# Delta attention's block product and merge: unpaired, with 96 weight columns, and queues drawn anew

## The reference

```python
def step(S, inp):
    qt, kt, vt, bt, gt = inp
    S = S * jnp.exp(gt)[..., None, None]
    for i in range(nh):                       # nh = 3
        ki, vi, bi = (kt[:, :, i], vt[:, :, i], bt[:, :, i])
        kS = jnp.einsum('bhd,bhde->bhe', ki, S)
        S = S + bi[..., None, None] * (ki[..., None] * (vi - kS)[:, :, None, :])
    o = jnp.einsum('bhd,bhde->bhe', qt, S)
    return (S, o)
```

## Time and profile before

| | us |
|---|---|
| median of three runs | 3138.93 |
| profiled execution | 3139.86 |
| its span, first to last instruction | 3138.0 |
| TensorE matmuls busy | 2919.0 (93%) |
| TensorE weight loads busy | 2241.5 (71%) |
| VectorE busy | 2486.9 (79%) |
| ScalarE busy | 2346.9 (75%) |
| GpSimd busy | 1977.9 (63%) |

### The profile page before, as it was taken

The page is one execution under the profiler, slowest core; times in us unless marked ns, Lnnn a source line. Parts: engine busy times, 40 slices in busy tenths (PEclk is TensorE's granted clock), DMA queues, the critical chain, the costliest instruction groups (busy, mean ns, idle before and its releaser), DMA issues. The chain is left out here.

```text
span 3138.0 us, 84065 instructions
## 1 busy us (share of the span) xinstructions
PE 2919.0 (93%) x27212; PEld 2241.5 (71%) x27212; DVE 2486.9 (79%) x5731; ACT 2346.9 (75%) x7723; POOL 1977.9 (63%) x3127
## 2 busy tenths in 40 slices
PE   5569999999999999999999999999987999768999
PEld 3448888888888888888888888888776444455444
DVE  5669999999999999999999999999754455594544
ACT  4769999999999999999999999999754443314443
POOL 1588888888888888888888888888831000100000
PEclk8779999999999999999999999999998999868999
DMA  5457777777777777777777777777532323002242
GB/s 108 123 147 179 190 187 180 180 184 174 184 187 191 182 182 182 178 179 182 193 184 182 183 179 182 180 189 181 154 96 75 152 102 152 10 3 78 107 160 115
DMA packets 588208, 482.91 MB, mean 154 GB/s; under 512 B 464784, under 2 KB 504368, under 8 KB 581632
## 3 DMA queue, kind: packets, MB, share of 16 engines
q1 hardware_dynamic: 579328, 474.39, 57.4%
q10 hardware_dynamic: 8448, 3.15, 0.4%
HBM read 285.53 MB, written 191.86 MB: 152 GB/s over the span
## 5 line engine op out<-in xcount | busy, mean ns | idle before, releaser
L953 DVE SCALAR_TENSOR_TENSOR conv_k<-PP,tk,conv_k 128x256 f32<-128x256 f32 x1536 | 718.5, 479 | 101.0 <-ACT conv_k L772 75.7
L953 DVE SCALAR_TENSOR_TENSOR conv_v<-PP,tv,conv_v 128x256 f32<-128x256 f32 x1152 | 540.5, 478 | 57.4 <-ACT conv_v L772 43.1
L710 POOL TENSOR_TENSOR X<-X,tmp 96x31 f32<-96x31 f32 (+15 forms) x992 | 534.3, 539 | 77.8
L707 POOL TENSOR_TENSOR tmp<-At,X 96x31 f32<-96x31 f32 (+15 forms) x992 | 486.7, 491 | 63.3 <-DMA At<-n_d 5.1
L1114 PE MATMUL PP<-xn,wk 128*128 128x268 f32 x1024 | 342.5, 418 | 41.4 <-DVE conv_k L953 29.7
L675 POOL TENSOR_TENSOR Sg<-S,gend 128x512 f32<-128x512 f32 x256 | 266.6, 1041 | 63.3 <-DVE S L912 63.3
L744 ACT ACTIVATE recA<-TG,es 96x128 f32<-96x128 f32 x1024 | 285.0, 367 | 6.3 <-DVE es L946 6.3
L693 POOL TENSOR_TENSOR rk<-ss,half 96x8 f32<-96x8 f32 x128 | 209.0, 1633 | 125.9 <-DVE ss L921 119.6
L1078 PE MATMUL RB<-rhs,Yf 96*96 96x128 f32 x2048 | 269.7, 274 | 18.7 <-DVE rhs L901 18.4
L772 ACT ACTIVATE conv_k<-PP,tk 128x256 f32<-128x256 f32 x512 | 245.2, 480 | 46.6 <-PE PP L1114 26.1
L1068 PE MATMUL RA<-S,kqgB 128*96 128x128 f32 x2048 | 276.1, 278 | 1.0 <-DVE S L912 1.0
(11 more groups left out here) (292 smaller groups left out, 6578.4 us busy)
## 6 DMA issues: line engine op xcount, KB each, us to landing
kqg_d<-kqgA SPq DMA_DIRECT2D x128, 512.0 KB, 6.4
kqgB<-kqg_d SPq DMA_DIRECT2D x128, 512.0 KB, 4.4
rec_d<-recA SPq DMA_DIRECT2D x128, 480.0 KB, 3.4
recB<-rec_d SPq DMA_DIRECT2D x128, 480.0 KB, 6.1
f1gates<-f1gates_d SPq DMA_DIRECT2D x24, 1024.0 KB, 6.8
f2gates<-f2gates_d SPq DMA_DIRECT2D x24, 1024.0 KB, 6.9
gdec<-gdec_d SPq DMA_DIRECT2D x128, 128.0 KB, 5.8
apk_d<-apkA SPq DMA_DIRECT2D x128, 128.0 KB, 3.3
```

Source lines behind the costliest of these rows:

```text
L707: nc.gpsimd.tensor_tensor(t, At[q % 2][:, j, j + 1:].unsqueeze(2).broadcast_to(sh), X[q % 2][:, j, 0:cols].unsqueeze(1).broadcast_to(sh), ...
L710: nc.gpsimd.tensor_tensor(x, x, t, ALU.subtract).then_inc(sub_ev, 1)
L953: return nc.vector.scalar_tensor_tensor(acc, src[:, :, j:j + SPAN], w[:, j:j + 1], acc, ALU.mult, ALU.add)
```

## The change

**Block product and merge.** `zm`, `wm` and `m3` run unit after unit. The weights of zm and wm are now 96 columns wide: a unit's 64 and the next unit's first 32, so that the output has 96 rows, of which the last 32 are never read. `apkB` and the buffer behind `Zt` get 32 more columns of zeros for the last unit. ZW has eight units on the same partitions. m3 writes 32 rows, with 32 weight columns. The copies are one per call and twice as large, two for `zev`.

```diff
-        ZW, RA, RB, SD = pb("ZW", [128, HU, 64]), ...
+        ZW, RA, RB, SD = pb("ZW", [128, U, 64]), ...
...
-                for u in paired():
-                    last = mm(spot(u, 0, 64), apkB[N % 2][:, u, :], Dd[N % 2][:, u, :], start=True, stop=True)
+                for u in range(U):
+                    last = mm(ZW[0:R, u, :], apkB[N % 2][:, 64 * u:64 * u + R], Dd[N % 2][:, u, :], start=True, stop=True)
                 last.then_inc(zm_mm, 1)
...
-                for u in paired():
-                    last = mm(spot(u, 0, 64), Zt[:, u, :], Yf[N % 2][:, u, BLK:R], start=True, stop=True)
+                for u in range(U):
+                    last = mm(ZW[0:R, u, :], ZtW[:, 64 * u:64 * u + R], Yf[N % 2][:, u, BLK:R], start=True, stop=True)
                 last.then_inc(wm_mm, 1)
...
-                for u in paired():
-                    last = mm(spot(u, 32, 64), Zt[:, u, :], Yf[N % 2][:, u, 64:96], start=True, stop=True)
+                for u in range(U):
+                    last = mm(ZW[0:32, u, 32:64], Zt[:, u, 0:32], Yf[N % 2][:, u, 64:96], start=True, stop=True)
                 last.then_inc(m3_mm, 1)
...
-                for p in range(2):
-                    nc.scalar.activation(half(Zt[32:64, :, 0:32], p), ZW[64 * p:64 * p + 32, :, 0:32], ACT.Copy, scale=-1.0)
-                    last = nc.scalar.activation(half(Zt[64:96, :, :], p), ZW[64 * p + 32:64 * p + 64, :, :], ACT.Copy, scale=-1.0)
-                last.then_inc(zev_ev, 1)
+                nc.scalar.activation(Zt[32:64, :, 0:32], ZW[0:32, :, 0:32], ACT.Copy, scale=-1.0)
+                nc.scalar.activation(Zt[64:96, :, :], ZW[32:64, :, :], ACT.Copy, scale=-1.0).then_inc(zev_ev, 1)
```

**Queues.** The loops run one pass longer, and the border of a pass lies elsewhere: f - 1 in a call below is what f was. On TensorE:

```diff
-                v_tile(c, 0)  v_tile(c, 1)  ktr(f - 1, 1)  ks(r, 0)  ktr(f - 1, 0)  zm(c)  ot(r - 1)
-                w_(r, 0)  v_tile(c, 2)  out(r - 1)  gate_tile(c)  sr(r, 0)  k_tile(f, 1)  o_(r, 0)
-                k_tile(f, 0)  wm(c)  ks(r, 1)  gram(f - 1, 0)  k_tile(f, 2)  w_(r, 1)  gram(f - 1, 1)
-                k_tile(f, 3)  o_(r, 1)  m3(c)  vtr(c, 1)  vtr(c, 0)  sr(r, 1)
+                ktr(f - 2, 1)  ks(r - 1, 0)  v_tile(c - 1, 2)  ot(r - 2)  ktr(f - 2, 0)  w_(r - 1, 0)
+                out(r - 2)  gate_tile(c - 1)  sr(r - 1, 0)  k_tile(f - 1, 1)  k_tile(f - 1, 0)  wm(c - 1)
+                ks(r - 1, 1)  gram(f - 2, 0)  k_tile(f - 1, 2)  gram(f - 2, 1)  k_tile(f - 1, 3)
+                w_(r - 1, 1)  o_(r - 1, 0)  m3(c - 1)  o_(r - 1, 1)  vtr(c - 1, 1)  v_tile(c, 0)
+                sr(r - 1, 1)  v_tile(c, 1)  zm(c)  vtr(c - 1, 0)
```

On ScalarE (the calls of a pass, new order):

```diff
+                osb_(r - 2)  ksum_(f - 2, 1)  tap0(c - 1, "v2")  ksum_(f - 2, 0)  wev(r - 1, 0)  gate_(c - 1)
+                vsilu(c - 1)  tap0(f - 1, "k1")  tap0(f - 1, "k0")  kr(f - 2, 0)  kr(f - 2, 1)
+                xt(*group_at(f - 1, 2 * GROUP + 1))  tap0(f - 1, "k2")  tap0(f - 1, "q")  w12(c - 1)
+                wev(r - 1, 1)  q2_(f - 2)  yev(c - 1)  mo_(r - 1, 0)  mo_(r - 1, 1)  tap0(c, "v0")
+                ksilu(f - 1)  qsilu(f - 1)  tap0(c, "v1")  zev(c)
```

On VectorE (new order; taps of different tiles stand between each other where they can):

```diff
+                tap2(c - 1, "v1")  rhs_(r - 1, 0)  og_(r - 2)  tap1(c - 1, "v2")  tap3(c - 1, "v1")
+                tap2(c - 1, "v2")  tap3(c - 1, "v2")  ss_(f - 2)  rinv_(f - 2)  step_(f - 2)  acc_(r - 2)
+                es_(f - 2)  sup(r - 1, 0)  tap1(f - 1, "k0")  tap2(f - 1, "k0")  tap1(f - 1, "k1")
+                tap3(f - 1, "k0")  tap2(f - 1, "k1")  tap3(f - 1, "k1")  rhs_(r - 1, 1)  ap(f - 2, 0)
+                tap1(f - 1, "k2")  ap(f - 2, 1)  tap2(f - 1, "k2")  tap1(f - 1, "q")  tap3(f - 1, "k2")
+                tap2(f - 1, "q")  tap3(f - 1, "q")  vr(c - 1, 1)  tap1(c, "v0")  sup(r - 1, 1)
+                tap2(c, "v0")  tap3(c, "v0")  tap1(c, "v1")  vr(c - 1, 0)
```

On GpSimd and SyncE:

```diff
+                sg(r - 1, 1)  subst(*group_at(f - 1, GROUP + 1), range(0, 6))  fo_(r - 1)  rk_(f - 2)  sg(r, 0)
+                x_zero(*group_at(f, 3))  subst(*group_at(f - 1, GROUP + 1), range(6, 12))  kqg(f - 1)
...
-                at_load(*group_at(f, GROUP + 1))  x_store(*group_at(f, 2 * GROUP + 1))  rec_load(c)  da_load(c + 1)
-                weights(*divmod(f, KSTEPS))  dec_load(f)  kqg_store(f - 1)  rec_store(f - 1)  ap_store(f - 1)
-                y_load(c + 1)
+                at_load(*group_at(f - 1, GROUP + 1))  dec_load(f - 1)  weights(*divmod(f + 1, KSTEPS))  tables(f + 1)
+                rec_load(c - 1)  x_store(*group_at(f - 1, 2 * GROUP + 1))  kqg_store(f - 2)  da_load(c + 1)
+                ap_store(f - 2)  rec_store(f - 2)  y_load(c)
```

```diff
-                nc.vector.tensor_tensor(kv[:, :, 0, :], kv[:, :, 0, :], end, ALU.mult)
-                nc.vector.tensor_tensor(rv[:, :, 1, :], rv[:, :, 1, :], mid, ALU.mult).then_inc(t_ev, 1)
-                dve.wait_ge(t_ev, ...)
-                nc.vector.tensor_tensor(fv[:, :, 1, :], fv[:, :, 1, :], mid, ALU.mult).then_inc(up_ev, 1)
+                nc.vector.tensor_tensor(r, r, mid, ALU.mult)
+                dve.wait_ge(kup_ev, kups[l, b] + 1)
+                nc.vector.tensor_tensor(f, f, mid, ALU.mult).then_inc(up_ev, 1)
...
+            def keys(l, b):
...
+                pool.wait_ge(up_ev, ups[l - 1, b] + 1)
+                pool.wait_ge(p_mm, products(l, b) + 1)
+                k = halves(kB, l, b)[:, :, 0, :]
+                nc.gpsimd.tensor_tensor(k, k, last_of_half(l, b, 1), ALU.mult).then_inc(kup_ev, 1)
```

More of the change, by code:

```diff
@@ L477, in half @@
             return t[:, hf * HU:(hf + 1) * HU]
[L479 to L483, removed]
         def of_cc(t, cc):
@@ L530, in wv_load, with tables @@
                 sp.dma_start(wo[h % 2][:, :], g.dram["Wo"][128 * h:128 * (h + 1), :]).then_inc(ld_wv[h % 2], 16)
+            def tables(h):
+                if 0 < h < NH:
+                    for b in range(B):
+                        keep_table(sp, h, b)
             def dec_load(N):
@@ L845, in w12 @@
                 need(act, wm_mm, N)
-                for p in range(2):
-                    last = nc.scalar.activation(half(Yf[N % 2][32:64, :, 64:96], p), ZW[64 * p + 32:64 * p + 64, :, 32:64], ACT.Copy)
-                last.then_inc(w12_ev, 1)
+                nc.scalar.activation(Yf[N % 2][32:64, :, 64:96], ZW[32:64, :, 32:64], ACT.Copy).then_inc(w12_ev, 1)
             def yev(N):
@@ L853, in yev @@
                 need(act, m3_mm, N)
-                for p in range(2):
-                    last = nc.scalar.activation(half(Yf[N % 2][0:32, :, 32:96], p), ZW[64 * p:64 * p + 32, :, :], ACT.Copy)
-                last.then_inc(yev_ev, 1)
+                nc.scalar.activation(Yf[N % 2][0:32, :, 32:96], ZW[0:32, :, :], ACT.Copy).then_inc(yev_ev, 1)
             def xt(q, k):
@@ L1675, in steps @@
                 yield "tile", i
-                for l in range(2):
-                    b, odd = divmod(i - 2 - l, 2)
-                    if not odd and 0 <= b < B - 1:
-                        yield "near", (l, b)
-            yield "near", (0, B - 1)
-            yield "near", (1, B - 1)
-            for l in range(2, LV + 1):
+                for x in WITHIN[i]:
+                    yield "near", x
+            done = [x for w in WITHIN for x in w]
+            for l in range(LV + 1):
                 for b in range(B):
-                    yield ("near" if l < MASKED else "far"), (l, b)
+                    if (l, b) not in done:
+                        yield ("near" if l < MASKED else "far"), (l, b)
         order = [x for kind, x in steps() if kind == "near"]
         near_no = {x: n for n, x in enumerate(order)}
-        ups = {}
+        ups, kups = {}, {}
         for kind, x in steps():
@@ L1880, in _ @@
                 spread(b)
-            for b in range(B):
-                far(LV, b)
+            for l, b in FAR:
+                far(l, b)
             for q in range(NG // 4):
@@ L1899, in _ @@
                 nc.gpsimd.memset(P[:, 4 * i:4 * i + 4, :, :], 0.0).then_inc(cleared, 1)
+            def keys(l, b):
+                if not l:
+                    return
+                pool.wait_ge(up_ev, ups[l - 1, b] + 1)
+                pool.wait_ge(p_mm, products(l, b) + 1)
+                k = halves(kB, l, b)[:, :, 0, :]
+                nc.gpsimd.tensor_tensor(k, k, last_of_half(l, b, 1), ALU.mult).then_inc(kup_ev, 1)
+            nc.gpsimd.memset(mhalf[:, :], -0.5).then_inc(mhalf_ev, 1)
+            pool.wait_ge(mhalf_ev, 1)
+            root(0)
+            for kind, x in steps():
+                if kind == "tile":
+                    root(x + 1)
+                else:
+                    keys(*x)
         @block.vector
```

287 lines of the change are left out of this document (151 added, 136 removed).

## The result

The changed kernel takes 3384.17 us (median of 4 runs, 3381.02 to 3388.69); the kernel before, run beside it, 3139.14. The ratio is 1.078, 95% interval 1.076 to 1.080: 7.8% slower, where 0.9% was forecast. The profiled span is 3379.1 us against 3138.0, 241.1 more.

What follows compares the result with a forecast made beforehand. TensorE's queue was taken to set the frame (16.9 us, waits adding 0.35). 3139.9 + 52 (full frames) + 4 (last frames) - 8 (prologue) - 21 (decay_attention) = 3166.9 us, 3166 on the median; 8-in-10 range 3115 to 3212.

Steps and rivals of the forecast that it cites:

- The products, +0.59 us a frame: TensorE's unpaired zm, wm and the three blocks in 32-column shape: 4.41 us a frame against 3.82, so +0.59.
- The long frame loses its 1.1 us, `sr` 0 waits 0.2: xt behind kr saves the long frame 1.1 us; sr 0 waits 0.2 us for ScalarE each frame; frame 17.7, +52 us total.
- I cost that at nothing, its cover is 0.1 us: VectorE's rhs, og and three taps before gate end together with TensorE's out: cost nothing, with 0.1 us of cover.
- unless an order makes them late: Opening bound: GpSimd, ScalarE and VectorE are off the frame's critical path unless their order makes them late.
- shares badly with VectorE: Prologue's bound: if GpSimd, doing the odd masks, shares badly with VectorE, the gain is -5 instead of -8 us.
- Rival C: GpSimd's late fo delays osb on ScalarE, so sr 0 waits 0.6 us; frame 18.15, total 3220 us; chance 0.15.
- Last frames: +4 forecast: In the eleven or so frames at the end, the longer zm lies in the chain through the state: +4 us.
- Prologue -8: Fewer SP stores in the prologue and odd masks on GpSimd end it earlier: -8 us, bounds -5 and -10.
- decay_attention: -21 forecast: k products move from VectorE to GpSimd, steps take 2.43 instead of 3.15 us: -21 us, bounds -10 and -26.
- The bound of -10: decay_attention's lower gain, -10 us, if steps inside the tiles delay the roots on GpSimd.

Runs made afterwards that it cites:

- the run with kqg moved: Changed kernel with GpSimd's kqg of step f - 2 right behind sg of chunk 1, instead of step f - 1 at the pass's end: 3158.28 us, ratio 1.005.
- kqg is in pieces: Changed kernel with kqg's key product in four pieces of 192 elements, kqg in its place: 3166.65 us with pauses between pieces, 3163.21 us without.
- whole products with pauses: Changed kernel with kqg's two products whole and in place, GpSimd waiting before the key product and between the products: 3187.3 us, ratio 1.014.
- the old loop with kqg in pieces: Kernel before with new tables (stores at SP's pass end), GpSimd masks and decay levels, plus kqg's key product in four pieces without pauses: 3149.35 us, ratio 1.003.
- two halves: Changed kernel with kqg's key product cut into two halves of 384 elements, without pauses: 3382.08 us.
- `xt` moved: Old loop, paired products, new tables (stores at SP's pass end), masks and decay levels; xt behind kr of half 1, x_store at pass end: 3162.73 us, ratio 1.007.
- paired products in the new queues: Changed kernel with the old paired zm, wm, m3 and their copies put back; new queues, tables and decay levels stay: 3415.1 us, ratio 1.088.
- kqg moved in the kernel before: Kernel before with kqg on GpSimd behind sg 0 and rk instead of ahead of both: 3457.92 us, ratio 1.103.
- sup 0 first: Changed kernel with VectorE's sup of chunk 0 ahead of ss, rinv, step, acc and es instead of behind them: 3676.61 us.

## Why the forecast was wrong

- **The products, +0.59 us a frame: right within 0.1.** The sixteen records of wm take 1.49 us, that is (1.49 - 0.246) / 15 = 83 ns from one to the next, where I had 85; m3's lie 32 ns apart, as forecast:

```profile
1010.46 1.49 PE L1206 MATMUL ZW<-Yf,ZtW 96*96 96x64 f32 x16
...
1019.90 0.67 PE L1214 MATMUL ZW<-Yf,ZtW 96*32 96x32 f32 x16
```

  In their new places, in the run with kqg moved, zm and wm take 1.33 each (1.36 forecast), and `o_` 0, m3 and `o_` 1 with their way in and out 2.52 - 0.87 = 1.65 (1.69 forecast). The sum is 4.31 instead of 4.41, +0.49 on the 3.82 of before:

```profile
1034.91 1.04 PE L1081 MATMUL RB<-rhs,Yf 96*96 96x128 f32 x8
...
1037.43 0.64 PE L1188 MATMUL TG<-ident,vt 128*96 128x128 f32 x4
...
1039.72 1.49 PE L1197 MATMUL ZW<-Dd,apkB 96*96 96x64 f32 x16
1041.05 0.60 PE L1188 MATMUL TG<-ident,vt 128*96 128x128 f32 x4
```

- **The long frame loses its 1.1 us, `sr` 0 waits 0.2: right in the sum.** `sr` 0 waits 0.27 us a frame for ws in the run with kqg moved. With kqg out of the way all frames are 17.70 us and 115 of them cost 52.6 us more than before; the forecast had 17.7 and +52. With the hold out of the way the total was measured at 3158, within the range.
- **The failed step is the one on VectorE** ("I cost that at nothing, its cover is 0.1 us"), and before it the sentence that GpSimd and VectorE are off the path "unless an order makes them late". I compared VectorE's order with TensorE's (rhs, og and the taps ahead of `gate`), and never with GpSimd's. The forecast used the fact that GpSimd "shares badly with VectorE" for a bound of the masks in the prologue and left it out where both queues were drawn anew. It was to be read before the run: kqg is the last call of GpSimd's pass, ss, step and es the first ones of VectorE's that read and write SBUF alone, and both follow the end of `qsilu`. A trace of the price was in the old profile too: es has a mean of 648 ns where an undisturbed one takes 430 (the one at 1012.06 us). Measured: the three operations take 2.05 us a frame more, and the full frames lose 275.0 - 52.6 = 222 us to it: about 135 as TensorE's waits and an estimated 67 as lower clock, which the forecast had at full; the last 20 were not followed.
- **Rival C** had GpSimd in it and the nearest time of all (3220), but by `fo` and `osb`. The long wait of `fo` is there as an effect: it goes when kqg is in pieces, with `fo` and `osb` where they were.
- **Last frames: +4 forecast, -10.4 measured.** Most are 14.6 us each, where before they were 14.9 to 17.8. I took the chain through the state as lengthened by zm; the new order shortens it, and more so with kqg early (170.1 us for twelve).
- **Prologue -8: the number, not its way.** The first `out` comes 8.0 us earlier. But SP issues the first loop table ahead of the first `dec_load`, which stands at 71.05 us against 72.53; TensorE's first tile of the loop starts 4.1 us earlier (68.46 against 72.58), and the rest came in the fill. In the other runs with this prologue the first `out` lies anywhere from 241.0 (whole products with pauses) to 250.0 us (the old loop with kqg in pieces), so a gain of anything from nothing to 9 us is borne out; that the changed kernel hits 8.0 is luck. What moves the fill was not followed.
- **decay_attention: -21 forecast, -15.1 measured.** Steps at the end are 2.43 us apart where they are undisturbed, as forecast. But with the k product on GpSimd, VectorE's products of r and F take 862 and 855 ns instead of 692, and the k product itself 1575 on average, not 1040 (the shortest take 1.07; what the hold adds to it and what its own access costs was not separated):

```profile
L1989 DVE TENSOR_TENSOR b_rF<-b_rF,b_F 128x512 f32<-128x512 f32 x28 | 24.1, 862 | 0.0
...
L1991 DVE TENSOR_TENSOR b_F<-b_F 128x512 f32<-128x512 f32 x28 | 23.9, 855 | 1.0 <-POOL b_kB L1921 1.0
...
L1921 POOL TENSOR_TENSOR b_kB<-b_kB,b_F 128x512 f32<-128x512 f32 x28 | 43.9, 1575 | 49.3 <-PE b_pair L1770 46.3 <-PE b_pair L1783 1.8 <-DVE b_F L1991 1.2
```

  28 times (0.170 + 0.162) is 9 us, more than the missing 6, so the same hold can account for it; no run took it apart. The bound of -10 that I gave named late roots, not this.

What stays open: ScalarE as the wall at 17.7 (above), what moves the fill, and why the tail is shorter. The best kernel measured is the old loop with the tables and decay levels of the change, 0.4% faster than before.

## What to carry to other kernels

When queues are redrawn, lay the VectorE and GpSimd queues beside each other and mark the operations that touch SBUF alone. Keep GpSimd's long products off VectorE's small scalars on a chain, or cut them up: an idle engine's order can cost more than the busy engine's work. A group whose count is unchanged and whose mean has grown is the first thing to look for in the profile after; the granted clock of the same stretch is the second, for a wait of TensorE can cost more than it lasts.

## What the runs showed of the hardware

- **Which operations are held.** In the changed kernel ss (one SBUF input, a scalar addition), step and es (two SBUF inputs) grow; `rinv`, a reciprocal from SBUF, stays at 0.20 us, and taps, rhs, ap, sup, vr and og, with an input in PSUM, keep their lengths. The Trainium skill ("SBUF — State Buffer", Who interferes with whom) has this list: VectorE contends with a GpSimd instruction that reads SBUF when it has two SBUF inputs or runs in a mode that uses both ports, and whoever is first holds the pair for the whole instruction. The trace agrees on the kinds, but not on how long.
- **How long.** It is not one instruction, as that page has it. Without pauses `ss` and es stand through the end of a subtraction and both products (`ss` 2.68 us in the case shown, es up to 3.03), and through two halves and the query product (2.81). A pause of some 0.08 us in GpSimd's queue, at a semaphore wait, lets VectorE in (1.71 us at most). Quarters of 192 elements let it in even without one (es at 1009.75 in that run takes 0.49 us while the pieces run), halves of 384 do not. And step, issued at 1030.01 us in the changed kernel, 0.03 us after kqg started, got in at the border between its two products (1.57 us). What decides at a border was not found.
- **Waits of TensorE and its clock.** From 300 to 2300 us the granted clock is 1.00 in the kernel before, with unpaired products alone, with kqg moved, in pieces or with pauses. It is 0.98 with `xt` moved and with paired products in the new queues, 0.97 in the changed kernel and with two halves, 0.95 with kqg moved in the kernel before, and 0.92 with sup 0 first, all runs in which TensorE waits far longer in a frame. Where the lower level follows a wait of 1.80 us (`xt` moved), the frame is 1.65 us longer than where it doesn't.
- **A long GpSimd instruction does not always hold.** `rk`, a power of 8 elements that takes 1.63 us, leaves VectorE's step beside it at 0.15 us in the kernel before. With kqg queued right behind rk, step is held from within rk (issued at 1009.16, rk ends at 1009.82) to the end of kqg's first product:

```profile
1008.19 1.63 POOL L693 TENSOR_TENSOR rk<-ss,half 96x8 f32<-96x8 f32 x1 [1.99 <-DVE ss L921]
1009.79 1.57 POOL L660 TENSOR_TENSOR kqgA<-kq,gdec 128x768 f32<-128x768 f32 x1
```

```profile
1009.16 2.23 DVE L937 TENSOR_TENSOR step_s<-rinv,beta 96x8 f32<-96x8 f32 x1
```
